# A four-layer gated decoder on one core: ternary feed-forward reordered with the next stage's small folds in it, first rows loaded in parts

## Chip, core and metric

One core of one Trainium2 chip runs the whole program in one launch. The metric is the device time in microseconds (us), lower is better. Engines are called by the profile's names: PE is TensorE (PEld its weight loads), DVE VectorE, ACT ScalarE, POOL GpSimd, SP the sync engine that issues the DMAs.

## The reference, cut to what matters

The input x has 16 sequences of 56 rows of 256 values. Four layers follow; each adds a gated attention and then a gated feed-forward, both on layer-normalised rows. The feed-forward of layer 1 is the ternary one:

```python
def h_bitlinear(x, w):
    xq = act_quant(fwht(x))       # Hadamard transform, then 8 bits per row: scale 127/max|x|, round, clip to -128..127
    wq = weight_quant(w)          # ternary weights, one scale per matrix
    return jnp.einsum('bsh,oh->bso', xq, wq)
gate = h_bitlinear(hidden_states, w_gate)   # 256 -> 1024
up = h_bitlinear(hidden_states, w_up)       # 256 -> 1024
return h_bitlinear(jax.nn.silu(gate) * up, w_down)   # 1024 -> 256
```

The attention of layer 2 needs, per head, the products of small matrices (`W_qr` with `W_kr`, and `w_kc_q` with `Wq`) before its queries can be computed; the kernel calls these products folds.

## The kernel before, in words

The 896 rows are 8 tiles of 112 rows. The program is a row of blocks with a barrier of all engines between two; in a block each engine runs its own list of instructions in order, and waits on semaphores that the others raise. The blocks that matter here are these.

`begin` (lines 355 to 391): SP loads x in one transfer, then the identity matrix and two rows of gates, then the weights of the first attention (`ahead.load`). DVE waits for all four of the first transfers (`came` at 64) and takes mean and variance of each tile (`take_moments`, lines 351 and 353), PE waits for the same and runs 8 matmuls that nobody reads (`keep_busy`, line 219). SP leaves the block only when all weights have landed.

`causal_attention` of layer 0 (from 418): POOL clears `values` (4096 words, line 478) and smaller buffers, then writes the masked keys (line 490), four `tensor_tensor` per pair of sequences, each kept until the scores two pairs before are done. DVE normalises the eight tiles (`scale_all`, line 267), PE turns each (line 310), ACT copies it (line 286), and PE then projects the queries (line 517).

`ternary_ffn` (from 1789). `rows(p)` on DVE scales two tiles of rotated rows (maximum, three small operations, two `tensor_scalar` that multiply and clip at 127, one that clips at -128 and adds the rounding constant). Then per tile t: PE computes gate and up (`inner`, eight matmuls, line 1864, four banks `ps_gu`), ACT takes silu of the gate half (line 1950), DVE multiplies with the up half (`product`, line 2013) and does the first level of a Hadamard transform of 1024 (`butterflies`, lines 1724 and 1725), POOL does two more levels (the same lines), PE turns the result (`turn_h`, 1877), ACT copies it (`take_h`, 1957), PE rotates it with a 128 x 128 Hadamard matrix (`rotate`, 1889), DVE quantises (`quantise` and `clip`, 2025 to 2039), ACT rounds to bf16 (1963), PE turns that (`turn_quantised`, 1899), ACT copies (1969), PE multiplies with the down weights (`down`, 1908), and DVE adds to x (`add`, 2043). `rotate`, `turn_quantised` and `down` each begin with three `keep_busy` matmuls. The order is written out by hand, and PE's is:

```python
                for i in range(2, NT + 3):
                    if i < NT:
                        inner(i)
                    if i < NT + 2:
                        turn_h(i - 2)
                        rotate(i - 2)
                    if i >= 3:
                        turn_quantised(i - 3)
                        down(i - 3)
```

On the side, POOL clears the buffers of the next stage's small weights `wqrT` and `wkrT` (line 172), and SP then loads these (six transfers, 1,024 KB) and two large ones (1,536 and 2,048 KB).

`queries_roped` of layer 2 (from 1161): PE first folds `wqrT` with `wkrT` in twelve steps into two halves of a PSUM bank (lines 1218 and 1221), ACT copies each to `z` (line 1275); only then PE folds the sixteen heads of `G` (line 1227), ACT takes the root for the norm (line 278) and casts `G` (line 1279), and DVE, after the moments (lines 253 and 256), takes the low part (line 1298), which lets PE go on four heads later.

## Time and profile before

| what | value |
|---|---|
| median of 3 runs | 1644.47 us (1644.42 to 1648.88) |
| the profiled execution | 1653.14 us, its span 1651.3 us, mean granted clock 0.976 |
| busy in the span | PE 1550.3, PEld 1239.0, DVE 906.1, ACT 648.8, POOL 668.3 us |
| `begin` and the attention of layer 0 up to the first scores | 0 to about 34 us |
| ternary feed-forward | about 645.6 to 745.6 us |
| roped queries of layer 2 | from 745.9 us |
| moved by DMA in the span | 154.47 MB, mean 94 GB/s |

Most of the span is the two long attentions of layers 1 and 2, which the change leaves alone. A time of the profile counts from the first instruction. A row of the timeline has the start, the length, the engine and the line, what is written and read, how many instructions were merged in it, and in brackets how long the engine had been idle and who ended that. "PEclk" is the granted TensorE clock as a share of 2.4 GHz, so 0.50 is 1.2 GHz.

### The profile page before, as it was taken

The page shows a single profiled execution, that of the slowest core. Times are in us where ns is not written, and L with a number is a line of the kernel's source. Part 1 is how long each engine was busy: PE and PEld are TensorE (multiplying, and loading weights), DVE is VectorE, ACT ScalarE, POOL GpSimd, SP SyncE. Part 2 cuts the span into 40 slices and gives each one's busy share as a digit, 9 for nine tenths or more (in the row PEclk, how much of TensorE's full clock was granted, in tenths as well). Part 3 has the DMA queues.
Part 4 walks back from the last instruction along what each step waited for, and adds up shares of the span by engine and source line. Part 5 has one row for each costly group of instructions (what it writes and reads, how often), then busy time and mean ns, then how long its engine had stood idle before and what let it go on. Part 6 is the DMA issues. An engine that isn't in the chain of part 4 may idle for free. (4 is left out here: it accounts for less than half of the span.)

```text
span 1651.3 us, 39610 instructions
## 1 busy us (share of the span) xinstructions
PE 1550.3 (94%) x17172; PEld 1239.0 (75%) x17184; DVE 906.1 (55%) x1648; ACT 648.8 (39%) x931; POOL 668.3 (40%) x482
## 2 busy tenths in 40 slices
PE   6889899999999998788998999999999999898998
PEld 3575688888888877676665888888888878645565
DVE  4950566665667626864555555565655253367212
ACT  3544344444444433344011544444454422144221
POOL 4405664465544100630975636644462011080101
PEclk9999899999999999998998999999999999999999
DMA  8006575644563122104123655355622030061402
GB/s 222 14 10 145 115 154 128 140 115 114 117 144 90 42 87 74 45 1 128 48 56 83 142 136 121 92 122 120 135 68 62 3 118 0 5 240 54 163 23 64
DMA packets 66413, 154.47 MB, mean 94 GB/s; under 512 B 14924, under 2 KB 44172, under 8 KB 65376
## 3 DMA queue, kind: packets, MB, share of 16 engines
q1 hardware_dynamic: 65472, 150.10, 36.2%
q8 instruction: 136, 2.23, 0.6%
q0 software_dynamic: 768, 1.84, 0.4%
q14 instruction: 37, 0.30, 0.1%
HBM read 87.51 MB, written 5.51 MB: 56 GB/s over the span
## 5 line engine op out<-in xcount | busy, mean ns | idle before, releaser
L1593 DVE TENSOR_REDUCE latent_psW<-latent_psW 128x1 f32<-128x500 f32 x654 | 418.1, 682 | 233.2 <-PE latent_psW L1488 232.7
L1571 ACT ACTIVATE latent_w<-latent_psS 125x896 f32<-125x896 f32 x384 | 351.7, 919 | 427.4 <-PE latent_psS L1506 423.8
L1516 PEld LDWEIGHTS latent_psO<-latent_val,latent_w 125*64 125x64 f32 x10752 | 323.8, 138 | 24.6 <-issue 11.1
L1516 PE MATMUL latent_psO<-latent_val,latent_w 125*64 125x65 f32 x10752 | 339.4, 223 | 0.0
L1505 PE MATMUL latent_psS<-latent_qA,latent_kA 128*125 128x448 f32 x768 | 290.6, 378 | 3.9 <-DVE latent_qB L1609 2.4
L1506 PE MATMUL latent_psS<-latent_qB,latent_kB 128*125 128x448 f32 x768 | 282.4, 368 | 0.0
L1488 PE MATMUL latent_psW<-latent_kA,latent_qA 128*128 128x500 f32 x654 | 214.5, 397 | 3.4 <-DMA latent_qA<-latent_qh 2.4
L1505 PEld LDWEIGHTS latent_psS<-latent_qA,latent_kA 128*125 128x125 f32 x768 | 143.6, 187 | 31.1 <-ACT latent_w L1571 4.6
L1506 PEld LDWEIGHTS latent_psS<-latent_qB,latent_kB 128*125 128x125 f32 x768 | 143.8, 187 | 19.9
L1488 PEld LDWEIGHTS latent_psW<-latent_kA,latent_qA 128*128 128x128 f32 x654 | 124.4, 191 | 20.3 <-DVE latent_psW L1593 5.8
L935 POOL TENSOR_TENSOR latent_rawT<-latent_rawT,latent_ropeT 128x1000 f32<-128x1000 f32 x48 | 110.8, 2334 | 34.0 <-DMA latent_rawT<-in_ctx_cols 22.0
L967 POOL TENSOR_TENSOR latent_val<-latent_raw,latent_turned_half 125x768 f32<-125x768 f32 x32 | 59.0, 1843 | 152.7 <-PE latent_psO L1516 150.2
L1452 POOL TENSOR_TENSOR latent_ql<-latent_q,latent_qh 128x448 fp32r<-128x448 f32 x32 | 36.4, 1141 | 156.0 <-ACT latent_qh L1562 155.9
L1318 POOL TENSOR_TENSOR q_u_roped<-q_u_roped 128x448 f32<-128x448 f32 x48 | 54.0, 1151 | 76.0 <-DVE q_u_roped L1308 75.8
L1308 DVE TENSOR_TENSOR q_u_roped<-q_ps_g,q_rope 128x448 f32<-128x448 f32 x96 | 53.2, 616 | 45.1 <-PE q_ps_g L1248 23.5
L958 POOL TENSOR_TENSOR latent_turned_half<-latent_raw,latent_rope 125x384 f32<-125x384 f32 x64 | 63.2, 1008 | 21.2 <-DMA latent_raw<-in_ctx 21.1
L1614 DVE RECIPROCAL latent_rec<-latent_psO 128x7 f32<-128x7 f32 x32 | 6.6, 205 | 115.0 <-PE latent_psO L1516 115.0
L950 POOL TENSOR_TENSOR latent_rawT<-latent_rawT,latent_high 128x1500 fp32r<-128x1500 f32 x16 | 54.3, 3391 | 18.6 <-ACT latent_high L979 18.6
L1673 PE MATMUL out_ps<-latent_fold,latent_q 128*112 128x256 f32 x256 | 59.1, 388 | 1.8 <-PEq L1399 1.8
L963 POOL TENSOR_TENSOR latent_raw<-latent_raw,latent_rope 125x768 f32<-125x768 f32 x32 | 59.1, 1848 | 2.4
L940 POOL TENSOR_TENSOR latent_rawT<-latent_rawT 128x500 f32<-128x500 f32 x48 | 59.3, 1263 | 0.0
L1673 PEld LDWEIGHTS out_ps<-latent_fold,latent_q 128*112 128x112 f32 x256 | 45.4, 181 | 11.6 <-issue 2.0
(399 smaller groups left out, 2201.7 us busy)
## 6 DMA issues: line engine op xcount, KB each, us to landing
latent_qA<-latent_qh SPq DMA_DIRECT2D x128, 112.0 KB, 2.6
latent_rawT<-in_ctx_cols SPq DMA_DIRECT2D x32, 375.0 KB, 5.2
latent_rawT<-in_ctx_cols SPq DMA_DIRECT2D x64, 187.5 KB, 5.8
latent_raw<-in_ctx SPq DMA_DIRECT2D x32, 375.0 KB
latent_kA<-latent_high SPq DMA_DIRECT2D x32, 375.0 KB, 4.2
latent_kB<-latent_high SPq DMA_DIRECT2D x32, 375.0 KB, 5.7
latent_kA<-latent_rawT SPq DMA_DIRECT2D x32, 375.0 KB, 6.2
experts_wgu<-in_L_gu SPq DMA_DIRECT2D x8, 1024.0 KB, 16.2
```

Of the source, the lines that this page charges most:

```text
L935: pool.tensor_tensor(x[:, :, at], x[:, :, at], self.ropeT[:, :, at], ALU.mult).then_inc(self.product, 1)
L940: pool.tensor_tensor(x[:, 0, at], x[:, 0, at], x[:, 1, at], ALU.add).then_inc(self.keys_roped, 1)
L958: last = pool.tensor_tensor(self.turned_half[:, :, lo:lo + 32], self.raw[b % 2][:, :, hi:hi + 32], self.rope[:, 1, :, lo:lo + 32], ALU.mult)
L963: pool.tensor_tensor(self.raw[b % 2][:, :, :], self.raw[b % 2][:, :, :], self.rope[:, 0, :, :], ALU.mult).then_inc(self.roped, 1)
L967: pool.tensor_tensor(self.val[b % 2][:, :, 0:DC], self.raw[b % 2][:, :, :], self.turned_half[:, :, :], ALU.add).then_inc(self.val_ready, 1)
L1488: pe.matmul((spare if alone and j % 2 else psW)[:, m, 0:THIRD], qA[u][:, j * 128:(j + 1) * 128], kA[u][:, n.part(m)], start=True, stop=Tru ...
L1505: pe.matmul(to[:, h, 0:GH], kA[u][:, at], qA[u][:, h * GH:(h + 1) * GH], start=True, stop=False)
L1506: last = pe.matmul(to[:, h, 0:GH], kB[u][:, at], qB[b % 2][:, h * GH:(h + 1) * GH], start=False, stop=True)
L1516: last = pe.matmul(sums[r:r + 64, c, :], w[t % ROUND][:, queries_of(c, r):queries_of(c, r) + 64], val[b % 2][:, t, :], start=(t == 0 and c ...
L1571: act.activation(w[t % ROUND][:, :].rearrange("p (h n) -> p h n", h=2), psS[0:KP, t % 2, :, 0:GH], ACT.Exp).then_inc(exp_done, 1)
L1593: dve.tensor_reduce(bank[:, THIRD + j:THIRD + j + 1], bank[:, 0:THIRD], mybir.AxisListType.X, ALU.max).then_inc(max_ready, 1)
L1673: last = pe.matmul(ps[0:TP, t % 2, 0:C], q[:, j, t * TP:(t + 1) * TP], fold[:, j, :], start=(j == 0), stop=(j == HP - 1))
```

## The change

Six edits.

1. `begin`: x comes in four transfers with a semaphore each, the identity between the first and the second; DVE takes the moments of a pair of tiles when its part is there, PE and ACT wait for the other three transfers.
2. `causal_attention`, layer 0: POOL no longer clears `values` first but between its fourth and fifth key product, and it begins the keys only when the eight normalised tiles are written (`norm.xn_ready`). Layer 3 keeps its order.
3. `ternary_ffn`, quantisation: the clip operations and one small operation per pair and per tile are left out, the scale being folded into the others; the product and the rounding constant are one `tensor_scalar`.
4. `ternary_ffn`, order: gate and up raise two semaphores, and silu waits for the gate alone; down of tile i-4 stands before rotate of tile i-2; the copies on ACT and the additions on DVE move accordingly; the last tile uses the banks of `ps_gu`; all `keep_busy` are left out but one of six before the last turn; all four `rows(p)` stand ahead of the first product.
5. The twelve folds of `wqrT` and `wkrT` move from `queries_roped` into `ternary_ffn`, six before gate(1) and six after the fourth turn of rows, on PE and ACT.
6. The small weights are loaded first and on a semaphore of their own.

```diff
@@ begin @@
-                sp.dma_start(g.x[:, :, :], d["x"].rearrange("(t p) c -> p t c", p=TP)).then_inc(came, 16)
-                sp.dma_start(g.ident[:, :], d["ident"]).then_inc(came, 16)
+                for p in range(NT // 2):
+                    sp.dma_start(g.x[:, 2 * p:2 * p + 2, :], rows[:, 2 * p:2 * p + 2, :]).then_inc(x_came[p], 16)
+                    if p == 0:
+                        sp.dma_start(g.ident[:, :], d["ident"]).then_inc(came, 16)
...
-                    take_moments(dve, g, t, came, 64, stats_done)
+                    take_moments(dve, g, t, x_came[t // 2], 16, stats_done)
@@ causal_attention, gpsimd @@
-                pool.memset(values[:, :, :, :, :], 0.0).then_inc(zeroed, 1)
+                if layer:
+                    pool.memset(values[:, :, :, :, :], 0.0).then_inc(emptied, 1)
...
+                if not layer:
+                    pool.wait_ge(norm.xn_ready, NT)
                 pool.wait_ge(taken, KV)
                 for n in range(2 * B):
                     b, c = n // 2, n % 2
+                    if n == 4 and not layer:
+                        pool.memset(values[:, :, :, :, :], 0.0).then_inc(emptied, 1)
@@ RopedWeights, new @@
+    def fold_tensor(self, pe, n):
+        k, t = n // 3, n % 3
+        flat = lambda v, e: self.wqrT[:, v, :, :, :].rearrange("p j e i -> p (j e i)")[:, e]
+        if n == 0:
+            pe.wait_ge(self.small_came, 16 * len(self.small_loads))
+        if n >= 2:
+            pe.wait_ge(self.z_ready, n - 1)
...
+        last.then_inc(self.z_done, 1)
+    def fold_scalar(self, act, n):
+        act.wait_ge(self.z_done, n + 1)
+        act.copy(self.z[:, n, :, :, :].rearrange("p v e n -> p (v e n)"), self.bank[n % 2][:, 0:256]).then_inc(self.z_ready, 1)
@@ queries_roped: the twelve fold steps on PE and their copies on ACT are gone @@
-                for n in range(3 * QUADS):
...
-                    act.copy(z[:, n, :, :, :].rearrange("p v e n -> p (v e n)"), ps_q[:, 0, n % 2, 0:256]).then_inc(z_ready, 1)
@@ ternary_ffn, tensor @@
+                for p in range(NPX - 1):
+                    rotate_rows(p)
                 turn_rows(0)
-                inner(0)
-                rotate_rows(2)
+                gate_part(0)
+                up_part(0)
+                rotate_rows(NPX - 1)
                 turn_rows(1)
-                rotate_rows(3)
                 turn_rows(2)
-                inner(1)
+                pe.wait_ge(x_taken, NT)
+                for n in range(0, 6):
+                    ahead.fold_tensor(pe, n)
+                gate_part(1)
+                up_part(1)
                 turn_rows(3)
-                for i in range(2, NT + 3):
+                for n in range(6, 3 * (NH // 4)):
+                    ahead.fold_tensor(pe, n)
+                for i in range(2, NT + 1):
                     if i < NT:
-                        inner(i)
-                    if i < NT + 2:
-                        turn_h(i - 2)
-                        rotate(i - 2)
+                        gate_part(i)
+                    turn_h(i - 2)
+                    if i < NT:
+                        up_part(i)
+                    if i >= 4:
+                        down(i - 4)
+                    rotate(i - 2)
                     if i >= 3:
                         turn_quantised(i - 3)
-                        down(i - 3)
+                turn_h(NT - 1)
+                down(NT - 3)
+                rotate(NT - 1)
+                for t in (NT - 2, NT - 1):
+                    turn_quantised(t)
+                    down(t)
@@ ternary_ffn, vector @@
-                    step(dve.tensor_scalar(r2[:, at], r2[:, at], 127.0, 1.0 / 32.0, ALU.mult, ALU.mult))
-                    between()
...
-                    dve.tensor_scalar(ys[:, u, :].rearrange("p (a n) -> p a n", a=2), ps_y[0:TP, :, :], r2[:, at], 127.0,
-                                      ALU.mult, ALU.min).then_inc(y_taken, 1)
+                    dve.tensor_scalar(ys[:, u, :].rearrange("p (a n) -> p a n", a=2), bank, r2[:, at], ROUND,
+                                      ALU.mult, ALU.add).then_inc(y_taken, 1)
...
-                    dve.tensor_scalar(ys[:, u, :], ys[:, u, :], -128.0, ROUND, ALU.max, ALU.add).then_inc(y_clipped, 1)
...
-                rows(0)
-                rows(1)
-                rows(2)
+                for p in range(NPX):
+                    rows(p)
                 product(0)
-                rows(3)
                 product(1)
-                for i in range(2, NT + 3):
+                for i in range(2, NT + 1):
                     if i < NT:
                         product(i)
...
+                    if i >= 4:
+                        add(i - 4)
+                    quantise(i - 2)
+                add(NT - 3)
+                quantise(NT - 1)
+                add(NT - 2)
+                add(NT - 1)
```

## Rows read from the trace of the kernel before

**Rows 1.** Waits of SP's queue, first 60 us: total us, times, longest

```profile
SPq L365 <- DMA xattn_w__6_54<-in_headmask: 6.4, 1, 6.4
...
SPq L365 <- PEq L365: 0.3, 1, 0.3
```

**Rows 2.** Timeline of the first 35 us: start us, us, engine, line

```profile
12.94 3.51 POOL L478 MEMSET xattn_values<- 128x4096 f32 x1 [12.49 <-POOLq L365]
...
18.32 8.28 POOL L490 TENSOR_TENSOR latent_q<-xattn_kT,xattn_w__6_54 128x512 f32<-128x512 f32 x8
...
24.83 8.15 PE L517 MATMUL xattn_ps_a<-all_xnT,xattn_w__3_51 128*128 128x448 f32 x16 [0.43 <-ACT all_xnT L286]
```

**Rows 3.** Line 267 in the first layer, 14 to 25 us: ns min/median/max

```profile
L267 DVE TENSOR_SCALAR all_xn<-all_x,xattn_ln_rstd,xattn_ln_shift x8: 394/1128/1590, 15.0 to 22.6; 112x256 f32<-112x256 f32 x8
```

**Rows 4.** Line 267 in the third layer, 758 to 763 us

```profile
L267 DVE TENSOR_SCALAR all_xn<-all_x,q_ln_rstd,q_ln_shift x8: 404/406/411, 759.2 to 761.5; 112x256 f32<-112x256 f32 x8
```

**Rows 5.** Windows: stretch, length, busy us by engine, PEclk, DMA share, GB/s

```profile
25.00:29.00 4.00, 4.00 (x6) 1.85 (x7) 0.00 (x0) 0.54 (x1) 1.60 (x2) 0.55 0.96 217
...
650.00:655.00 5.00, 4.38 (x30) 3.44 (x29) 4.35 (x14) 1.98 (x3) 0.00 (x0) 1.00 1.02 170
```

**Rows 6.** Timeline, one turn of the ternary loop on PE and ACT

```profile
699.07 1.80 PEld L1889 LDWEIGHTS ffn_ps_y<-ffn_w__82_8816,ffn_hT 128*112 128x112 f32 x16 [0.74 <-ACT ffn_hT L1957]
...
701.47 0.51 PEld L1899 LDWEIGHTS ffn_ps_t<-ffn_w_identb,ffn_yq 112*128 112x128 bf16 x8
...
702.17 0.91 ACT L1969 COPY ffn_yqT<-ffn_ps_t 128x896 bf16<-128x896 bf16 x1 [2.11 <-PE ffn_ps_t L1899]
...
703.13 0.83 PEld L1908 LDWEIGHTS ffn_ps_t<-ffn_w_wb,ffn_yqT 128*112 128x112 bf16 x8 [0.46 <-ACT ffn_yqT L1969]
...
703.94 1.53 PEld L1864 LDWEIGHTS ffn_ps_gu<-ffn_w_wb,ffn_xqT 128*112 128x112 bf16 x8
...
705.97 1.12 ACT L1950 ACTIVATE ffn_h<-ffn_ps_gu,ffn_su 112x1024 f32<-112x1024 f32 x1 [2.90 <-PE ffn_ps_gu L1864]
...
706.99 0.90 ACT L1957 COPY ffn_hT<-ffn_ps_t 128x896 f32<-128x896 f32 x1
```

**Rows 7.** Line 1275, the copies of the twelve folds: ns min/median/max, first and last start

```profile
L1275 ACT COPY q_z<-q_ps_q x12: 372/372/373, 746.6 to 753.2; 128x256 f32<-128x256 f32 x12
```

**Rows 8.** Timeline, start of the roped queries

```profile
745.91 2.71 DVE L253 BATCH_NORM_STATS2 all_stats<-all_x 112x6 f32<-112x256 f32 x8 [0.32 <-PEq L1819]
...
748.54 0.62 DVE L256 BATCH_NORM_AGGREGATE all_mv<-all_stats 112x2 f32<-112x6 f32 x8
...
755.07 1.60 ACT L1279 CAST q_G<-q_ps_g 128x384 fp32r<-128x384 f32 x4
```

**Rows 9.** Timeline: third turn of rows, gate and up of tile 2, product of tile 2

```profile
660.33 0.37 PE L1853 MATMUL ffn_ps_t<-ffn_w_identb,ffn_xq 112*128 112x112 bf16 x4 [1.54 <-ACT ffn_xq L1938]
...
669.60 3.63 PE L1864 MATMUL ffn_ps_gu<-ffn_w_wb,ffn_xqT 128*112 128x512 bf16 x8 [1.38 <-DVE ffn_h L2013]
...
674.42 1.29 DVE L2013 SCALAR_TENSOR_TENSOR ffn_h<-ffn_ps_gu,ffn_su,ffn_h 112x1024 f32<-112x1024 f32 x1 [3.51 <-ACT ffn_h L1950]
```

**Rows 10.** Costliest lines, 698.2 to 715.9 us, two tiles: count, busy, mean ns

```profile
L1725 POOL TENSOR_TENSOR ffn_h<-ffn_h 112x512 f32<-112x512 f32 x4 | 5.1, 1271 | 0.3
...
L2013 DVE SCALAR_TENSOR_TENSOR ffn_h<-ffn_ps_gu,ffn_su,ffn_h 112x1024 f32<-112x1024 f32 x2 | 2.6, 1283 | 0.4 <-ACT ffn_h L1950 0.4
...
L1724 DVE TENSOR_TENSOR ffn_h<-ffn_h 112x512 f32<-112x512 f32 x2 | 1.4, 692 | 0.1
```

**Rows 11.** Timeline, a GpSimd and a VectorE butterfly at once

```profile
675.02 1.27 POOL L1725 TENSOR_TENSOR ffn_h<-ffn_h 112x512 f32<-112x512 f32 x1
...
675.74 1.10 DVE L1724 TENSOR_TENSOR ffn_h<-ffn_h 112x512 f32<-112x512 f32 x1
```

**Rows 12.** Timeline of the tail: product of tile 7 and the last addition

```profile
715.99 1.28 DVE L2013 SCALAR_TENSOR_TENSOR ffn_h<-ffn_ps_gu,ffn_su,ffn_h 112x1024 f32<-112x1024 f32 x1 [0.19 <-ACT ffn_h L1950]
...
745.11 0.48 DVE L2043 SCALAR_TENSOR_TENSOR all_x<-ffn_ps_t,ffn_s,all_x 112x256 f32<-112x256 f32 x1 [4.87 <-PE ffn_ps_t L1908]
```

More of the change, by code:

```diff
@@ L360, in begin @@
         came = a.sem("came")
+        x_came = [a.sem(f"x_came{p}") for p in range(NT // 2)]
         stats_done = a.sem("stats_done")
@@ L374, in _ @@
                 ahead.wait(sp)
+                sp.wait_ge(came, 48)
             @block.tensor
             def _(pe):
-                pe.wait_ge(came, 64)
+                pe.wait_ge(came, 48)
                 keep_busy(pe, g, ps[:, 0:128], 8)
@@ L1272, in _ @@
             def _(act):
-                for n in range(3 * QUADS):
-                    act.wait_ge(z_done, n + 1)
-                    act.copy(z[:, n, :, :, :].rearrange("p v e n -> p (v e n)"), ps_q[:, 0, n % 2, 0:256]).then_inc(z_ready, 1)
                 norm.root(act)
@@ L1977, in _ @@
                 take_rows(2)
+                for n in range(0, 4):
+                    ahead.fold_scalar(act, n)
+                round_rows(3)
+                for n in range(4, 6):
+                    ahead.fold_scalar(act, n)
                 silu(1)
-                round_rows(3)
                 take_rows(3)
-                for i in range(2, NT + 3):
+                for n in range(6, 3 * (NH // 4)):
+                    ahead.fold_scalar(act, n)
+                for i in range(2, NT + 1):
+                    if i >= 4:
+                        take_quantised(i - 4)
                     if i < NT:
                         silu(i)
-                    if i < NT + 2:
-                        take_h(i - 2)
+                    take_h(i - 2)
                     if i >= 3:
                         round_quantised(i - 3)
-                        take_quantised(i - 3)
+                take_quantised(NT - 3)
+                take_h(NT - 1)
+                for t in (NT - 2, NT - 1):
+                    round_quantised(t)
+                    take_quantised(t)
             @block.vector
@@ L2579, in program @@
             clear_semaphores(nc)
-            ahead = roped_weights(nc, g, d)
+            ahead = RopedWeights(nc, g, d)
             ternary_ffn(nc, g, w, ahead)
+            ahead.small.close()
             w.ctx.close()
```

201 lines of the change are left out of this document (105 added, 96 removed).

## The prediction

> **What bounds the kernel now.** The change touches three stretches, and I read each at the wait that ends last in it.
>
> The start. The view of SP's own waits shows that SP held the first block open: it waited 6.4 us for the last weights of the first attention and only 0.3 us more at the barrier [rows 1]; the next block opened at 12.94. The single load of x, for which DVE waits, is therefore only just behind. In the next block GpSimd clears `values` and then writes keys, 12.94 to 26.6, and in just that time DVE normalises eight tiles [rows 2]: they take 1128 ns (median, 1590 at most) where the same operation takes 406 ns in a stretch in which GpSimd does nothing [rows 3, 4]. The projection of the queries starts behind the last tile at 24.83 and takes 8.15 us, part of it at a granted clock of 0.55, after a stretch in which PE had waited for DVE between tiles [rows 2, 5].
>
> The ternary loop. In the timeline one tile takes 8.87 us (two products of DVE lie so far apart), and no engine is full. The loop closes over PE and ACT, because PE takes its list in order [rows 6]: from rotate's start 699.07 to the turn 701.47 it is 2.40 (keep-busy matmuls among it), to ACT's copy 0.70, to down 0.96, to gate and up 0.81, to silu 2.03, to the copy of the next tile 1.02, and that copy ends at 707.88, 0.9 later. Together 8.8. The work on DVE and POOL hangs beside it.
>
> The roped queries. ACT's twelve copies of folds start from 746.6 to 753.2, and the first cast of `G` follows at 755.07, although the moments are there at 749.16 [rows 7, 8].
>
> **Begin.** Three more issues on SP, about 0.5 us each, lie ahead of the weights, but the transfers run far behind the issues. The moments end some 4 us sooner, and SP's wait for the weights then ends the block: it saves the 0.2 to 0.3 by which SP came first. Taken: 0.2; bounds -0.5 (the issues delay the weights) to 0.5.
>
> **Keys behind the normalised rows.** DVE's eight tiles go from 1128 to 406 ns each, or 0.33 from start to start [rows 4]: 15.0 to 17.8. Then the pair of PE and ACT paces the turns: 0.41 on PE and 0.35 on ACT over two buffers give 0.43 a tile (estimate), the last copy ends at 20.7 instead of 24.8, so 4.1 saved. PE has no gaps to speak of in that time, so I take the projection at full clock, 16 times 0.376, 6.1 instead of 8.15: 2.0 more. GpSimd's keys: it began at 18.32 because it cleared first; now it begins at 17.9. Four keys take 4.1, the clearing 3.5 and the next four 4.1 [rows 2]: ready at 22.0 and 29.7. The first scores then want theirs at 27.6, the second at 30.6. Both are covered, the second by only 0.9. The clearing ends at 25.6, its reader comes near 31. Four transfers of folding weights wait for POOL's next clearing and now leave 3 us sooner; nobody waits. Taken: 6.1; bounds 4.0 (the clock falls as before) and 6.5.
>
> **The ternary stage, entry.** No product stands between the four `rows`, and each loses a small operation and a clip, some 0.6 a pair. The third turn of rows was at 660.33 [rows 9]; I put it at 658.0 (estimate). Then twelve fold steps, 0.59 each by the copies' starts [rows 7], gate and up of tile 1 (1.6), gate of tile 2, the turn of h and up (0.8, 0.8, 1.2): 658.0 + 7.1 + 1.6 + 2.8 = 669.5 for product 2, which stood at 674.42 behind matmuls at half clock (3.63 for eight, against 1.89 at full) [rows 6, 9]. Saved: 4.9. The folds are covered by POOL's 5.4 us for tile 0, which PE awaits anyway; without that cover they cost their 7.1. Their six small loads, 1,024 KB, go first from about 650 at the 170 GB/s of that window [rows 5], so they land near 656.5, 1.5 before fold 0. If they come at 661, all shifts by 3.
>
> **The steady loop.** Gate before turn, and down before rotate, cut PE's ring: its own work is 1.62 + 0.8 + 1.73 + 0.45 + 0.81 = 5.4 a tile, all keep-busy gone. DVE's list is product 1.32, two butterflies 1.34, addition 0.40, maximum 1.27, two small 0.38, write 1.19, small 0.24 = 6.1 (lengths by product and butterfly [rows 10], maximum and write taken like the product for their 1024 elements). POOL's is four times 1.345, 5.4. All three fit below 8.87, so what counts is who stands in whose way. With DVE at 6.1 a tile, its two butterflies fall on the end of POOL's work on the tile before. The one place where they met shows what then happens: POOL's ran 675.02 to 676.29, DVE's began at 675.74 and lasted 1.10 instead of 0.69, it ended 0.55 after POOL's [rows 10, 11]. So I let POOL's 5.4 and DVE's 1.4 exclude each other: 6.8 a tile. From product 2 to product 7 that is 34.0 instead of 41.6 (715.99 - 674.42 [rows 9, 12]): 7.6 saved. Ends: 6.1, if only that one row was slow, and 8.87.
>
> The Trainium skill, page "SBUF — State Buffer", section "Who interferes with whom", has this as a rule: a VectorE instruction with two SBUF inputs and a GpSimd instruction that reads SBUF use one port pair, and the second to start fully blocks until the first is through. The row above agrees. Read to the letter it gives the 6.8; without it the sum would be 3.5 us lower over five tiles.
>
> **The tail.** From product 7 on the last tile is a plain chain: product and blocked butterflies 3.5, POOL 5.4, turn 1.0, copy 0.95, rotate 2.05, maximum to write 2.95, round 1.2, turn 0.7, copy 0.95, down 1.2, that is 19.9 instead of 29.1 [rows 6, 10, 12], because tiles 5 and 6 no longer stand in line for `x_done` and the keep-busy: 9.2 saved. The last addition comes at 669.5 + 34.0 + 19.9 = 723.4. Stage: 21.7.
>
> **Roped queries.** With the folds gone, ACT loads its table during the moments and takes the root when they end, 3.26 after the stage's start, so the first cast of `G` comes at about 3.5 instead of 9.16 [rows 8]: 5.6 saved of the 7.2 removed. But PE now idles 2 us after four heads, and once more during the normalisation; I take 1.0 back for a fall of the clock. Taken: 4.6; bounds 3.0 and 5.7.
>
> **Sum.** 0.2 + 6.1 + 21.7 + 4.6 = 32.6. On the profiled execution (1653.14, span 1651.3) that gives 1620.5; it lies 8.7 above the median of the runs, and I take the difference off the median: 1644.47 - 32.6 = 1611.9, so 1612.
>
> **Rivals.** A measurement of this kernel can tell 0.3%, 4.9 us, from no change.
>
> Forecast (0.60): as summed.
>
> No exclusion (0.14): DVE alone sets 6.1 to 6.2; 3.5 less in the loop, 1 in the tail, 1607. For it: elsewhere DVE's product and write lie beside POOL at full speed. Against: [rows 11].
>
> The gains come in part (0.20): the small loads are late (3), the clock falls in the folds, in `G` or in the projection (2 each), or POOL and DVE block each other in both directions (0.4 a tile, 2 in all): 1612 + 8 = 1620. For it: the eight matmuls of tile 2 ran at half clock after PE had stood almost idle, and PE will idle in places again. Against: it takes all of them at once.
>
> PE at half clock all through the ternary stage (0.04), because keep-busy held it up: eight gate and up matmuls took 3.63 against 1.89 [rows 6, 9], so 5.4 a tile become 10.4, 1.5 above the 8.87 of now, 12 over eight tiles; the twelve folds cost 6.5 more. The stage is then 18.5 slower, the rest saves 8 to 9: about 1654. It decides once a tile takes over 8.87, that is if PE is slow for more than two thirds of it. Against: gaps in the new list stay below 1 us, and a PE busy for 4.38 of 5 us held the full clock [rows 5]. The Trainium skill, page "TensorE: Matmul & The Clock Gate", Part 1, states that throttled is the default and that activity lifts it; the trace agrees in both directions, and this rival is that rule at its worst.
>
> No change to speak of (0.02): a later stage takes the gain back; nothing in the profile shows such a link, as the blocks are parted by barriers.
>
> **How the numbers follow.** Faster by over 0.3% holds the first three: 0.94. Slower 0.04, same 0.02. The range leaves out 0.2 at most: down to 1603 (no exclusion, no fall of the clock, 1606, less 3 for the spread of the runs, which was 4.5 before), up to 1624 (partial gains 1620, plus 4).
>
> **What would show it.** Line 267 near 400 ns in the first layer and keys starting at 17.9. The projection at 16 x 0.38. Products of tiles 3 to 7 spaced 6.8, with the first butterfly longer than 0.69 and ending just behind a POOL operation; 6.1 and 0.69 would be the second case. Fold 0 at 658 without a wait for a DMA. The stage about 78 us long instead of 99.7. First cast of `G` 3.5 after the stage's start. A PEclk of 0.5 in the ternary loop, or a product spacing above 8, would make the prediction wrong.

## Result and the profile after

The changed kernel takes 1624.05 us (median of 4 runs, 1620.69 to 1630.3) beside 1646.68 for the kernel before on the same chip (1644.42 to 1650.83). The ratio is 0.9846, 95% interval 0.9822 to 0.987: 25.4 us faster (21.4 to 29.3) where 32.6 were forecast. The time stands on the upper edge of the range, 1624, while the median of before is 2.2 above the 1644.47 that the forecast started from. The same kernel timed again beside the last experiments gave 0.9846 once more. One of the ten executions of the kernel with the keys alone took 3059.65 us, in a slow state, and is not in its ratio.

The profiled execution took 1626.06 us, its span 1624.3 (before 1653.14 and 1651.3). From here on, times inside a stage are counted from the stage's own start (a plus sign), because what is gained earlier shifts everything behind it.

The start, in the timeline of the kernel after (start, duration, engine, line, operation; in the bracket the idle time before and what ended it):

```profile
7.00 0.43 SPq L190 DMA_DIRECT2D xattn_w__6_54<-in_headmask  x1
9.31 0.18 DVE L353 BATCH_NORM_AGGREGATE all_mv<-all_stats 112x2 f32<-112x6 f32 x1
13.92 0.11 POOL L486 MEMSET xattn_qT<- 128x16 f32 x1 [13.48 <-POOLq L366]
15.99 2.67 DVE L267 TENSOR_SCALAR all_xn<-all_x,xattn_ln_rstd,xattn_ln_shift 112x256 f32<-112x256 f32 x8
18.80 4.04 POOL L501 TENSOR_TENSOR latent_q<-xattn_kT,xattn_w__6_54 128x512 f32<-128x512 f32 x4 [3.09 <-DVE all_xn L267]
21.93 7.97 PE L528 MATMUL xattn_ps_a<-all_xnT,xattn_w__3_51 128*128 128x448 f32 x16 [0.44 <-ACT all_xnT L286]
30.77 0.38 PE L547 MATMUL xattn_ps_a<-xattn_maskb,xattn_identb 128*128 128x512 bf16 x1 [0.86 <-ACT xattn_qT L625]
```

The moments end at 9.5 instead of 12.7, but the next block opens at 13.92, not at 12.94 [rows 2]: nobody needed them sooner, and the last weights now come later. The eight normalisations take 2.67 us together instead of 8.70, and GpSimd's keys begin right behind them. The projection starts 8.0 behind the block's opening instead of 11.9, yet it takes 7.97, not the 6.1 of the forecast.

The ternary stage starts at 642.44. Its entry, the same view:

```profile
656.15 0.71 PE L1200 MATMUL ffn_ps_y<-q_small_wkrT,q_small_wqrT 128*128 128x128 f32 x4 [0.29 <-DVE ffn_xs L2074]
657.56 2.08 PE L1200 MATMUL ffn_ps_y<-q_small_wkrT,q_small_wqrT 128*128 128x128 f32 x8
...
664.27 1.25 PE L1200 MATMUL ffn_ps_y<-q_small_wkrT,q_small_wqrT 128*128 128x128 f32 x8
...
669.36 1.28 DVE L2083 SCALAR_TENSOR_TENSOR ffn_h<-ffn_ps_gu,ffn_su,ffn_h 112x1024 f32<-112x1024 f32 x1 [3.25 <-PE ffn_ps_gu L1900]
```

and the granted clock (PE busy, PEclk, DMA share, GB/s) there, with one stretch of the loop:

```profile
642.00:645.00 3.00, 2.52 (x8) 0.74 0.00 0
657.00:660.00 3.00, 3.00 (x20) 0.52 0.99 421
663.00:666.00 3.00, 3.00 (x33) 1.00 0.00 0
675.00:678.00 3.00, 2.32 (x25) 1.00 0.00 0
```

Fold 0 (656.15) waits for DVE's rows and not for a load: the last small load landed at 654.12. The clock was down at the stage's start as well (0.74). The same eight fold matmuls take 2.08 at a granted clock of 0.52 (near 1.2 GHz) and 1.25 at 1.00 (2.4 GHz). Product 2 comes at +26.9; before it was +28.8 [rows 9].

One turn of the steady loop, and ahead of it DVE's first butterfly of an earlier one:

```profile
677.10 1.63 DVE L1755 TENSOR_TENSOR ffn_h<-ffn_h 112x512 f32<-112x512 f32 x1
...
690.27 1.27 POOL L1756 TENSOR_TENSOR ffn_h<-ffn_h 112x512 f32<-112x512 f32 x1
690.85 1.24 DVE L1755 TENSOR_TENSOR ffn_h<-ffn_h 112x512 f32<-112x512 f32 x1
692.12 0.69 DVE L1756 TENSOR_TENSOR ffn_h<-ffn_h 112x512 f32<-112x512 f32 x1
692.89 1.28 POOL L1755 TENSOR_TENSOR ffn_h<-ffn_h 112x512 f32<-112x512 f32 x1 [1.35 <-DVE ffn_h L1756]
```

DVE's first butterfly begins under GpSimd's last operation, which ends at 691.54, and is through 0.55 later; the second takes its 0.69; GpSimd starts again after 1.35 idle. 5.35 and 1.35 are 6.7, and products 3 to 7 stand 6.68, 7.07, 6.67 and 6.68 apart (8.87 before, from product 4 on). In the turns before the first addition (0.48) DVE has less to do, its butterfly begins earlier and takes 1.63, and the spacing is the same: there the exclusion sets the pace and not DVE's list. The 7.07 is the turn in which the first addition comes in. From product 7 (702.88) to the last addition (724.21) it is 21.3. The stage lasts 82.6 instead of 100.3, barriers included: 17.8 saved.

The roped queries start at 725.01:

```profile
728.51 1.60 ACT L1310 CAST q_G<-q_ps_g 128x384 fp32r<-128x384 f32 x4
735.83 4.17 PE L1262 MATMUL q_ps_g<-q_w__93_9153,q_w__94_9154 128*128 128x192 f32 x24 [2.05 <-DVE q_G_low L1329]
```

The first cast of `G` is at +3.5, where 9.16 stood [rows 8]. The first wide matmul (of the query projection) is at +25.6 instead of +33.2.

### The profile page after: what moved, and what is told of

It is laid out like the page before. It is cut to its first block and busy times, and to the rows that moved or that the text cites. A ratio compares the mean times of both kernels' runs of the same rounds, so it can differ in the third digit from the quotient of the medians.

```text
span 1624.3 us, 39337 instructions
## 1 busy us (share of the span) xinstructions
PE 1530.7 (94%) x17028; PEld 1221.2 (75%) x17040; DVE 891.4 (55%) x1624; ACT 649.1 (40%) x931; POOL 667.8 (41%) x482
## 5 line engine op out<-in xcount | busy, mean ns | idle before, releaser
L1547 PEld LDWEIGHTS latent_psO<-latent_val,latent_w 125*64 125x64 f32 x10752 | 323.9, 138 | 25.2 <-issue 11.6
L1536 PEld LDWEIGHTS latent_psS<-latent_qA,latent_kA 128*125 128x125 f32 x768 | 143.4, 187 | 31.1 <-ACT latent_w L1602 4.6
L1339 DVE TENSOR_TENSOR q_u_roped<-q_ps_g,q_rope 128x448 f32<-128x448 f32 x96 | 53.2, 617 | 45.7 <-PE q_ps_g L1282 24.1
```

What stands on the lines that cost most here:

```text
L1536: pe.matmul(to[:, h, 0:GH], kA[u][:, at], qA[u][:, h * GH:(h + 1) * GH], start=True, stop=False)
L1547: last = pe.matmul(sums[r:r + 64, c, :], w[t % ROUND][:, queries_of(c, r):queries_of(c, r) + 64], val[b % 2][:, t, :], start=(t == 0 and c ...
```

## Experiments

Each kernel was timed against the kernel before (medians of before 1649.2 to 1650.44 us beside them). "Cost" below is the difference to the ratio of the changed kernel, 0.9846, times 1650: a thousandth is 1.65 us, and the intervals reach 2.5 to 5.5 us to either side. Against the changed kernel only the clip and the keep-busy below are clear of noise by their times alone; for the others the time is a hint and the trace decides.

**x in one load again** (`begin` as before).

```diff
-                for p in range(NT // 2):
-                    sp.dma_start(g.x[:, 2 * p:2 * p + 2, :], rows[:, 2 * p:2 * p + 2, :]).then_inc(x_came[p], 16)
+                sp.dma_start(g.x[:, :, :], d["x"].rearrange("(t p) c -> p t c", p=TP)).then_inc(came, 16)
```

> The changed kernel with its first block as before: x in one load, moments behind it. Theory (issue order): the last weights land some 7 us after SP has issued them, and three issues fewer in front put that issue back from 7.0 to 5.6 us; the next block opens at 12.9 to 13.0 instead of 13.9, all later steps keep their distances, total 1.0 us below the changed kernel. Rival A (bytes): the landing is set by the volume, the block opens at 13.9 as in the changed kernel and the total stays. Rival B (moments): DVE's moments, which begin only when all of x is there, end last and the block opens later than 13.0.

Ratio 0.9849 (0.9818 to 0.988). In its timeline the last weights are issued at 5.60 and the block opens at 12.75; the moments end at 12.5. That is the theory's opening, but no gain shows in the total. All traces together say more. With one load the block opened at 12.94, 12.75, 12.65 and 12.56; with four parts at 13.92, 12.97, 14.80, 13.69, 13.37, 13.14, 13.07, 12.65 and 13.05. The means are 12.7 and 13.4, but the ranges overlap, and the changed kernel's second profile opened at 12.65 with its last weights issued as late as 6.98. That loading in parts costs 0.7 is a hint and not shown.

**x issued by ACT** (and no longer by SP).

```diff
+                for p in range(NT // 2):
+                    act.dma_start(g.x[:, 2 * p:2 * p + 2, :], rows[:, 2 * p:2 * p + 2, :]).then_inc(x_came[p], 16)
                 act.wait_ge(came, 48)
```

> The changed kernel with the four loads of x issued by ACT instead of SP, beside SP's loads of weights. Theory (issue order on SP sets the landing of the last weights): SP issues the last weights at about 5.1 us instead of 7.0, the next block opens near 12.5 instead of 13.9, total 1 to 1.5 below the changed kernel. Rival A (the volume sets it; the changed kernel's other executions opened between 13.0 and 14.8 with the same issues): opening anywhere from 12.9 to 14.8, total unchanged. Rival B (two queues at once delay x): DVE's moments end last and open the block after 13.

Ratio 0.9841 (0.9815 to 0.9867). SP issued its last weights at 5.61, and the block opened at 13.09. So an earlier issue alone doesn't bring the landing forward by as much: rival A. What sets it (order, volume, chance) stays open.

**The keys alone, on the kernel before.**

```diff
+                if not layer:
+                    pool.wait_ge(norm.xn_ready, NT)
                 pool.wait_ge(taken, KV)
...
+                    if n == 4 and not layer:
+                        pool.memset(values[:, :, :, :, :], 0.0).then_inc(emptied, 1)
```

> The kernel before with one part alone: in the first layer GpSimd waits for the normalised rows before its keys, and clears the values after four keys. Theory: the eight normalisations fall from 1128 to about 400 ns each, the projection of the queries starts 4.1 us sooner after the block's opening (11.9 to about 7.9) but still takes 8 us because the clock falls; the first scores come 4.0 us sooner and the total is 4.0 below the kernel before. Rival A (the forecast on record): the projection runs at full clock, 6.1 us, and 6.1 are saved. Rival B: part of the gain of the changed kernel in this stretch came from its moments being done early; alone the keys save under 3.

Ratio to before 0.9988 (0.9973 to 1.0003), so 2 us, with an interval that takes in no change. In the trace the normalisations are short again, but now the first matmuls of the block run at half clock and the projection at full:

```profile
12.84 5.55 PE L514 MATMUL xattn_ps_a<-xattn_w__2_50,xattn_w__1_49 128*128 128x512 f32 x8 [1.00 <-PEq L365]
22.29 6.28 PE L523 MATMUL xattn_ps_a<-all_xnT,xattn_w__3_51 128*128 128x448 f32 x16 [0.44 <-ACT all_xnT L286]
```

The eight took 3.91 in the profile of before and the projection 8.15 [rows 2]. The first scores come +16.6 behind the opening (20.9 before, 16.9 in the changed kernel).

**The keys undone, on the changed kernel** (the same lines taken out of it).

> The changed kernel with GpSimd's clearing and keys back beside the normalisation. Theory (GpSimd and DVE shut each other out there): the eight normalisations take 1128 ns each again, the projection starts 11.9 after the block's opening instead of 8.0, the first scores 18.8 to 20.9 instead of 14.9, total 4 to 6 above the changed kernel. What it tells besides: whether the projection at half clock (8.15 us) belongs to this slow normalisation, with PE waiting between tiles (then first scores at 20.9), or falls there by chance (then 6.28 us and 19.0).

Ratio 0.9855 (0.9836 to 0.9874), a cost of 1.5, not clear of noise. The timeline of this kernel shows why it is so little:

```profile
13.24 5.56 PE L513 MATMUL xattn_ps_a<-xattn_w__2_50,xattn_w__1_49 128*128 128x512 f32 x8 [1.24 <-PEq L366]
15.13 5.57 DVE L267 TENSOR_SCALAR all_xn<-all_x,xattn_ln_rstd,xattn_ln_shift 112x256 f32<-112x256 f32 x8
19.51 8.09 POOL L495 TENSOR_TENSOR latent_q<-xattn_kT,xattn_w__6_54 128x512 f32<-128x512 f32 x8 [0.97 <-ACT xattn_kT L608]
22.70 6.28 PE L522 MATMUL xattn_ps_a<-all_xnT,xattn_w__3_51 128*128 128x448 f32 x16 [0.44 <-ACT all_xnT L286]
```

PE's first eight matmuls fell to half clock, so GpSimd got its last operand at 19.43 and wrote keys only from 19.51; by then seven of the eight normalisations had begun, and DVE took 5.57 for the eight, not 8.70. The first scores stand at +16.8, as in executions with the keys moved and the same fall. The collision that the forecast priced from one trace is thus worth 0 to 6 us by the traces, depending on where the clock falls.

**The folds and their small loads back in the roped queries.**

```diff
-                for n in range(0, 6):
-                    ahead.fold_tensor(pe, n)
                 gate_part(1)
                 up_part(1)
                 turn_rows(3)
-                for n in range(6, 3 * (NH // 4)):
-                    ahead.fold_tensor(pe, n)
...
+                for n in range(3 * QUADS):
+                    act.wait_ge(z_done, n + 1)
+                    act.copy(z[:, n, :, :, :].rearrange("p v e n -> p (v e n)"), ps_q[:, 0, n % 2, 0:256]).then_inc(z_ready, 1)
                 norm.root(act)
```

> The changed kernel with the twelve folds and their small loads back at the start of the roped queries. Theory (the folds lie on PE's path in the ternary entry): product 2 comes 2.5 to 4 us sooner after the stage's start than the 26.9 of the changed kernel, because PE reaches the turn of tile 0 when GpSimd has it ready instead of 2.8 later and gate 1 is not queued behind six folds; the spacing of products 3 to 7 stays 6.7; the first cast of G comes 9.2 after the roped stage's start instead of 3.5, the next step 7.5 later. Total 3.5 to 5 above the changed kernel. Rival A (forecast: GpSimd's 5.4 us for tile 0 cover the folds): product 2 stays at 26.9 and the total is 7.5 above. Rival B (PE colder without the folds): matmuls of tile 2 at half clock, product 2 at 27 or later.

Ratio 0.9883 (0.985 to 0.9916), a cost of 6.1. Product 2 is at +25.4, the first cast at +9.16, the first wide matmul, that is the first of the query projection, at +31.5 (+25.6 in the changed kernel). So the roped queries pay 5.9 and the ternary stage gets back 0 to 1.5: the two kernels with folds at full clock (x in one load, and the changed kernel's second profile) have product 2 at +25.46 as well. The folds are free where PE keeps its clock, as the forecast said; in the changed kernel's own profile they cost 1.5, the fall of the clock among them.

**Gate of tile 1 ahead of most folds** (on PE; ACT's list follows).

```diff
-                for n in range(0, 6):
+                for n in range(0, 2):
                     ahead.fold_tensor(pe, n)
                 gate_part(1)
                 up_part(1)
+                for n in range(2, 6):
+                    ahead.fold_tensor(pe, n)
                 turn_rows(3)
```

> The changed kernel; in the ternary entry only two folds stay ahead of gate and up of tile 1, the other ten come behind. Theory (product 1 is late, 19.5 us after the stage's start at full clock and 20.9 with a fall of it, because six folds stand before it; GpSimd then waits 1.8 us for tile 1): product 1 comes at 17 to 18, GpSimd goes from tile 0 to tile 1 without a gap, product 3 and all after it come 1 to 2 sooner after the stage's start; total 1 to 2 below the changed kernel. Rival A (PE's sum of work sets product 2 whatever the order): product 1 sooner, products 2 to 7 unchanged at 25.4 (26.9 where the clock falls in the folds) and on. Rival B (the folds behind gate 1 delay the turn of tile 0): products 2 and on later than in the changed kernel.

Ratio 0.986 (0.9832 to 0.9889), a cost of 2.3 or none. Product 1 comes 5.0 behind product 0 (5.6 in the kernels whose folds ran at full clock), product 2 comes 13.4 behind it (13.1 in the changed kernel's profile, where the clock fell too), product 3 19.1 (19.5). Beyond product 1 at most 0.4 is gained: rival A.

**Half of the product left in PSUM.**

```diff
-                    dve.scalar_tensor_tensor(out=h[:, u, :].rearrange("p (n m) -> p n m", n=2), in0=ps_gu[0:TP, 2:4, :],
...
+                        last = dve.scalar_tensor_tensor(out=ps_gu[0:TP, 3, :] if n else half, in0=ps_gu[0:TP, 2 + n, :],
+                                                        scalar=su[:, 1, t:t + 1], in1=half, op0=ALU.mult, op1=ALU.mult)
...
+                    low, high = h[:, u, 0:512], ps_gu[0:TP, 3, :]
+                    step(dve.tensor_tensor(h2[:, u, 0:512], low, high, ALU.add))
```

> The changed kernel; in the ternary loop DVE's product is made in two halves, the second of which stays in PSUM, so that DVE's two butterflies read one operand from SBUF and one from PSUM instead of two from SBUF. Theory (DVE's butterflies with two SBUF operands and GpSimd's shut each other out): the first butterfly falls from 1.25 to 1.6 us to about 0.7 and no longer ends behind a GpSimd operation; the spacing of products 3 to 7 falls from 6.7 to 6.1 to 6.3 (DVE's own list), the last tile gains 0.6 more, total 2.5 to 4 below the changed kernel. Rival A (the order of PE and ACT sets the pace): the butterflies get short, DVE waits longer elsewhere, spacing stays 6.7. Rival B (the slow butterfly is GpSimd's load on SBUF as such, whatever DVE reads): the butterflies stay at 1.2 or more.

Ratio 0.9822 (0.9789 to 0.9855), 4.0 gained, not clear of noise by itself. DVE and GpSimd at the same place of its loop:

```profile
691.51 0.75 DVE L2085 SCALAR_TENSOR_TENSOR ffn_h<-ffn_ps_gu,ffn_su,ffn_h 112x512 f32<-112x512 f32 x1
692.30 0.76 DVE L2085 SCALAR_TENSOR_TENSOR ffn_ps_gu<-ffn_ps_gu,ffn_su,ffn_h 112x512 f32<-112x512 f32 x1
693.09 0.69 DVE L2094 TENSOR_TENSOR ffn_h<-ffn_h,ffn_ps_gu 112x512 f32<-112x512 f32 x1
...
692.26 1.27 POOL L1756 TENSOR_TENSOR ffn_h<-ffn_h 112x512 f32<-112x512 f32 x1
```

The butterfly of 693.09 lies half under GpSimd's operation (to 693.53) and takes 0.69. The products stand 5.99, 5.98, 6.37, 6.38 and 6.38 apart, 31.1 for the five instead of 33.5 in the profile of the changed kernel and 34.1 in its second. The tail takes 19.5, without a fall of the clock; of that gain 0.3 at most is the edit's, as the same tail without the edit takes 19.8 at full clock. All 16 butterflies of this trace take 0.69. The exclusion goes with DVE's second operand in SBUF; the rest of DVE's list then sets 6.4, of which 0.2 is the product's second instruction.

The Trainium skill, page "SBUF — State Buffer", section "Who interferes with whom", says that a VectorE instruction with at most one SBUF input, outside the two-port modes, doesn't contend with GpSimd. This trace agrees: 0.69 against 1.24.

**The clip back in the loop.**

```diff
+                    dve.wait_ge(y_taken, t + 1)
+                    dve.tensor_scalar(ys[:, u, :], ys[:, u, :], -128.0, ROUND, ALU.max, ALU.add).then_inc(y_clipped, 1)
```

> The changed kernel with the second, clipping pass of DVE over the 1024 quantised values of a tile back in the loop (0.79 us in the trace of before). Theory (DVE's list is full at 6.7 us a tile, the 0.55 of its blocked butterfly among them): spacing of products 3 to 7 from 6.7 to 7.4 or 7.5, the last tile 0.8 longer, the total 4 to 6 above the changed kernel. Rival A (the ring of GpSimd's 5.35 and DVE's two butterflies 1.35 sets the pace and DVE has room): spacing stays 6.7, only the tail is longer, total within 1.5. Rival B (DVE a little late shifts its butterflies clear of GpSimd, which removes the blocking): spacing 6.9 to 7.0, total 1 to 2 above.

Ratio 0.9886 (0.9867 to 0.9905), a cost of 6.6. From product 3 on the spacing is 7.50, the theory's. Its rows are the surprise:

```profile
695.66 1.27 POOL L1755 TENSOR_TENSOR ffn_h<-ffn_h 112x512 f32<-112x512 f32 x1
696.14 1.34 DVE L2103 TENSOR_SCALAR ffn_ys<-ffn_ys 112x1024 f32<-112x1024 f32 x1
697.01 1.60 POOL L1756 TENSOR_TENSOR ffn_h<-ffn_h 112x512 f32<-112x512 f32 x1
697.64 1.28 DVE L2083 SCALAR_TENSOR_TENSOR ffn_h<-ffn_ps_gu,ffn_su,ffn_h 112x1024 f32<-112x1024 f32 x1
698.96 0.69 DVE L1755 TENSOR_TENSOR ffn_h<-ffn_h 112x512 f32<-112x512 f32 x1
```

DVE runs 0.8 later, its butterfly is clear of GpSimd (0.69), but now the clip, from SBUF to SBUF with one operand, meets GpSimd and takes 1.34 instead of the 0.78 that most turns of before have for it (0.69 where GpSimd stood still). And GpSimd pays too: its operation of 697.01 begins under the clip and takes 1.60 instead of 1.27, as one does under the clip of each of six tiles. The block moved; it did not go. The tail is 24.1, 2.8 longer, with a granted clock of 0.75 and 0.68 in the two stretches of 6 us from 706 on.

**Keep-busy back in the loop** (three calls each before the rotations, the turns of quantised rows and the down projections of the loop).

```diff
+                        keep_busy(pe, g, ps_y[:, 0, 0:128], 3)
                     pe.wait_ge(hT_ready, t + 1)
...
+                    keep_busy(pe, g, ps_t[:, 1, 0:128], 3)
                     pe.wait_ge(yqT_ready, t + 1)
```

> The changed kernel with three keep-busy calls put back in front of each rotation, each turn of quantised rows and each down projection of the ternary loop (0.83 us for each three in the trace of before). Theory (they cost what they last, because the new order fills PE): PE's own list grows from 5.4 to 7.9 us a tile, the spacing of products 3 to 7 goes from 6.7 to about 7.9, and the total is 6 to 9 above the changed kernel (1630 to 1633). Rival A (they lie in PE's waits for DVE and GpSimd, 1.3 us a tile): spacing 6.7 to 7.0, total unchanged; then the gain of the loop is the new order's alone. Rival B (they hold the clock and pay for themselves in the tail): total at or below the changed kernel.

Ratio 0.9912 (0.9888 to 0.9936), a cost of 10.9. The last three products are 8.28 to 8.29 apart, 0.4 more than the 7.9 of PE's sum; PE is busy for 5.7 to 5.9 of every 6 us there, and DVE waits 1.1 us a tile for its rotation. The tail takes 24.6.

```profile
693.19 0.94 PE L219 MATMUL ffn_ps_t<-all_ident 128*128 128x128 f32 x6
693.96 1.04 PE L1958 MATMUL ffn_ps_t<-ffn_w_wb,ffn_yqT 128*112 128x256 bf16 x8
694.83 0.83 PE L219 MATMUL ffn_ps_y<-all_ident 128*128 128x128 f32 x6
695.50 1.91 PE L1935 MATMUL ffn_ps_y<-ffn_w__82_8821,ffn_hT 128*112 128x128 f32 x16
697.25 0.83 PE L219 MATMUL ffn_ps_t<-all_ident 128*128 128x128 f32 x6
697.45 1.23 DVE L2097 TENSOR_REDUCE ffn_r<-ffn_ps_y 112x1 f32<-112x1024 f32 x1 [1.12 <-PE ffn_ps_y L1935]
```

PE needs none of it to keep its clock in the loop: from 666 to 708 the changed kernel has 1.00 without. No run takes keep-busy out of the old order, so how much of the loop's gain is the new order's and how much only the missing keep-busy isn't shown.

**The addition between product and butterflies.**

```diff
                                              op0=ALU.mult, op1=ALU.mult).then_inc(product_done, 1)
+                    between()
                     dve.wait_ge(product_done, t + 1)
```

> The changed kernel; in the ternary loop DVE's addition of tile i-4 stands between its product and its butterflies of tile i, in the time in which the first butterfly would be blocked by GpSimd, instead of behind them. Theory (the tail is 1.4 longer than forecast because PE stands 1.5 us before the turn of tile 6, waiting for that addition, and then runs down(5) and the rotation of tile 6 at half clock): the turn of tile 6 starts 1.5 to 1.8 sooner, the tail from product 7 to the last addition falls from 21.3 to 19 to 20; the spacing stays 6.7, because GpSimd's 5.35 and the two butterflies of DVE still exclude each other. Total 1.5 to 2.5 below the changed kernel. Rival A (the butterflies then start later and GpSimd with them): spacing 7.1, total 1 to 2 above. Rival B (GpSimd's last tile is the tail's limit): tail 20.5 to 21.3, total unchanged.

Ratio 0.9843 (0.9825 to 0.9861): no difference that can be timed. From product 3 on the spacing is 6.67 to 6.69, without the one of 7.07, and the tail 20.1. PE in the tail (turn of tile 6, down of tile 5, rotation of tile 6), first of this kernel, then of the changed kernel's second profile, then of the kernel with the keys undone, whose ternary code is the changed kernel's:

```profile
701.48 0.96 PE L1922 MATMUL ffn_ps_t<-all_ident,ffn_h 112*128 112x112 f32 x8 [1.04 <-POOL ffn_h L1756]
703.43 1.08 PE L1956 MATMUL ffn_ps_t<-ffn_w_wb,ffn_yqT 128*112 128x256 bf16 x8 [0.99 <-ACT ffn_hT L2018]
704.72 2.00 PE L1933 MATMUL ffn_ps_y<-ffn_w__82_8821,ffn_hT 128*112 128x128 f32 x16 [0.21 <-DVE ffn_ys L2101]
```

```profile
700.88 0.96 PE L1922 MATMUL ffn_ps_t<-all_ident,ffn_h 112*128 112x112 f32 x8 [1.50 <-DVE all_x L2106]
702.84 1.96 PE L1956 MATMUL ffn_ps_t<-ffn_w_wb,ffn_yqT 128*112 128x256 bf16 x8 [0.99 <-ACT ffn_hT L2018]
704.58 2.71 PE L1933 MATMUL ffn_ps_y<-ffn_w__82_8821,ffn_hT 128*112 128x128 f32 x16
```

```profile
702.00 0.96 PE L1916 MATMUL ffn_ps_t<-all_ident,ffn_h 112*128 112x112 f32 x8 [1.50 <-DVE all_x L2100]
703.95 1.08 PE L1950 MATMUL ffn_ps_t<-ffn_w_wb,ffn_yqT 128*112 128x256 bf16 x8 [0.99 <-ACT ffn_hT L2012]
704.87 1.91 PE L1927 MATMUL ffn_ps_y<-ffn_w__82_8820,ffn_hT 128*112 128x128 f32 x16
```

In the second, PE stood 1.50 for the addition, and its next two steps took 1.96 and 2.71 instead of 1.08 and 2.00. In the third it stood the same 1.50, kept its clock (1.08 and 1.91), and the tail took 19.8. So the wait for the addition costs the tail nothing and doesn't by itself bring the fall. The turn itself comes only 0.5 sooner after product 7, not the 1.5 expected: GpSimd is then the one it waits for. Nor does the edit hold the clock: the kernel with three edits below has the early addition too, and there it fell.

**The changed kernel again.**

> The changed kernel unaltered, as the yardstick for the two others on the same chip and for the falls of the clock. Theory (the three stretches at half clock in its first profile, the projection 7.97 instead of 6.28 us, the rows 1.47 and the folds 1.46, are not fixed to these places): the second profile has at least one of them at full clock, product 0 at 12.4 or 13.8 and product 2 at 24.0, 25.5 or 26.9 after the stage's start. Rival (they belong to this program): all three lie where they lay, product 2 at 26.9.

Ratio 0.9846 (0.9827 to 0.9864). The projection took 6.28, but the block's first matmuls ran at half clock; product 0 is at +13.8, product 2 at +25.5. So the falls aren't fixed to the program.

**Three edits together** (x in one load, half of the product in PSUM, the addition early).

> The changed kernel with three edits together: x in one load, half of the product left in PSUM for DVE's butterflies, and the addition between product and butterflies. Theory: each keeps its own gain: the first block opens 0.9 sooner (12.8), the spacing of products 3 to 7 is 6.0 to 6.4 (1.6 to 2.4 in all), the tail from product 7 is 19.5 or less; the ternary stage takes 75 to 78 us instead of 80.2 to 82.6; total 4 to 6 below the changed kernel. Rival A (clock): a PE that idles more in the shorter loop falls to half clock there, and the stage stays above 79. Rival B: addition and butterflies in a row fill DVE, spacing 6.4 and no gain in the tail, total 3 below.

1619.87 us, ratio 0.9825 (0.9803 to 0.9847), against 0.9846 for the changed kernel beside it: faster by 3.5 to 4.7, with intervals that overlap. The block opens at 12.56, spacing 5.98 to 6.25, stage 78.2 with a tail of 21.2 in which the clock fell (0.72 from 700 to 706). By its ratio it is the fastest against before together with the PSUM edit alone, from which it can't be told.

## Where the clock fell

The same code in different executions, by the timelines. Full-clock values stand first; a cell with another number has a fall in it.

| stretch | at full clock | with a fall | fell in |
|---|---|---|---|
| opening of the block to first scores, keys moved | 14.9 to 15.2 | 16.6 to 17.9 | 5 of 12 traces |
| stage start to product 0 | 12.4 | 13.8 | 8 of 12 |
| product 0 to product 2 (folds as in the change) | 11.6 | 13.1 | 2 of 10 |
| product 7 to last addition | 19.5 to 20.1 | 21.2 to 21.5 | 7 of 10 |
| last six heads of `G` | 4.17 | 5.8 to 5.9 | 6 of 14 |

The first row counts the traces with the keys moved, the second those with the ternary order of the change. The third leaves out the two with another order of folds, the fourth the two with the clip or keep-busy back. Three of the ten in the fourth row have other edits in the loop (half of the product in PSUM 19.5, the addition early 20.1, both 21.2); of the seven without, six fell, and the kernel with the keys undone took 19.8. In the stretch to product 0 the granted clock tells them apart: 0.53 in the first 3 us of the kernel with one load (13.8), 1.00 in the kernel with keep-busy in its loop (12.4), with the same code there. The changed kernel's first profile has a fall in the first four rows, together 6.3 us.

## Why the prediction was right or wrong

**Direction and most of the mechanism** were right: faster, at 0.9846, by the ternary stage and the roped queries, as named. What the keys give isn't clear of noise in the total, and the first block gave nothing. The outcome lies nearer to the rival that had 0.20, the gains in part (1620, that is 24.5 saved), than to the sum that had 0.60. That rival named the falls of the clock in the projection and in the folds, which came, and late small loads, which didn't. That 1624.05 falls on the edge of the range and not beyond it is luck: leaving out a single one of the four executions moves the median by 2 us.

**Begin** (0.2, bounds -0.5 to 0.5): no gain came. The opening moved back by 1.0 in the two profiles and by 0.7 on average over the traces, which puts the step "the transfers run far behind the issues" in doubt. But it ran from 12.65 to 14.80 with the same issues, and the two runs on it show no gain in time, so the cause stays open.

**Keys behind the normalised rows** (6.1): mis-sized. The rows are as forecast: normalisation 407 ns, start of the projection 3.9 sooner (4.1), and where the clock held, the projection took 6.28 (6.1) and the scores came 6.0 sooner than in the profile of before. But the profile of before was a dear execution. With keys and normalisation in collision the scores stand at +20.9 there and at +16.8 in the other trace of it, and the timed runs give 2.0 (on the kernel before) and 1.5 (on the changed one). The step that failed is the price taken from a single execution, with its own fall of the clock in it. By the middle values this is 4 of the missing 7; both runs have intervals that reach from no gain to over 4 us.

**Ternary entry** (4.9): at full clock product 2 comes at +24.0 (four traces); the forecast's 669.5 is +23.9. That it fits so well is partly luck: the third turn of rows came at +11.6 and not at +12.4, and from there it took 12.4 and not 11.5. In the profile there are two falls, 1.5 each, and 1.9 was saved. The guard against that was in the rival "gains in part", which named the clock and the folds.

**Steady loop** (6.8 a tile, 34.0 for five): 33.5, and 34.1 where all stood at full clock. The exclusion was shown by taking one SBUF operand away: the butterflies fell from 1.24 or more to 0.69. With it DVE is busy for 5.8 of every 6 us, so that the 0.8 of the clip came through at once. The forecast that DVE and GpSimd would fit at 6.1 "if only that row was slow" is refuted.

**Tail** (19.9): 21.3 in the profile, 19.8 where PE kept its clock with the same ternary code. The sum was right for a PE at full clock. The step "plain chain" failed where the clock fell: the down projection of tile 5 and the rotation of tile 6 (1.96 and 2.56 instead of 1.08 and 1.91) then hold PE, and the turn of tile 7, the chain's next link, starts at 713.21 although GpSimd was through with that tile at 711.57. Counted from product 7 it comes 1.5 later than at full clock. PE's wait for the addition of tile 4 is in both and costs nothing.

**Folds, small loads:** free at full clock, no wait for a load. Right, though the margin was small: at full clock the last load landed at +11.3 to +11.6 and fold 0 began at +12.2.

**Roped queries** (4.6, of which -1.0 for the clock): 5.7 to the first cast, and 5.5 to 6.0 to the first wide matmul where the last six heads of `G` ran at full clock in both (+25.6 to +25.9 beside +31.4 to +31.5). The two profiles show 7.6, because the six heads were at half clock in that of before and not in the other. The fee for the clock is a matter of chance: the heads fell in 5 of 11 traces with the folds moved, with the first wide matmul then at +27.4 or +27.5, and in 1 of 3 without. Timed, the move of the folds is worth 6.1.

**The sum.** Timed or measured by stage it is now: keys 1.5 to 2, ternary stage with its folds 17.8 (the two profiles; 19.5 as the mean of five traces against two), roped queries 5.9 to 7.6, begin 0 to -1.0, together 24 to 29 beside the measured 25.4. At full clock everywhere the ternary stage is 78.8 long (the kernel with the keys undone; forecast 78), so the forecast described an execution without a fall, and among the traces only the kernel with keep-busy back has none in the five stretches of the table. From the first wide matmul to the end it is 871.8 to 876.7 us in the traces, with the same code behind it: 872.3 to 873.2 in the three kernels whose folds are not moved, 874.8 as the mean of the eleven others. Whether the change costs 2 us there is open.

## What to carry over

Price a collision or a projection from more than one execution if the granted clock is below 1 anywhere near it: one fall is 1.5 to 2 us, as large as a good edit. Where two engines exclude each other over SBUF, look at how many operands of DVE lie there: leaving one in PSUM parted them here, while moving DVE's list by 0.8 only moved the block to the next instruction. In the tail the fall cost 1.5 because the chain's next link stood in PE's line behind the slow matmuls: look there first. Whether transfers that gate a barrier gain by an earlier issue isn't shown here.

## What was not expected

The falls come in the same places of the program but not in each execution: the same ternary entry has product 2 at +24.0, +25.5 or +26.9. The stretch between two stages that no edit touches (from the first scores to the ternary stage) took 607.5 to 613.9 us.

DVE's one-operand pass from SBUF to SBUF was stretched by GpSimd as well, 0.78 to 1.34 and 0.41 to 1.13. DVE pays more often, but not alone: GpSimd's butterfly took 1.59 to 1.60 instead of 1.27 once in the second profile of the changed kernel and seven times with the clip back, each time begun while a stretched operation of DVE was still under way. In the trace of before one took 1.69 (from 688.90) behind a clip that had begun at 688.76 and kept its 0.69: there GpSimd alone paid. The Trainium skill has this too, in the same section of "SBUF — State Buffer": `tensor_scalar` can enter a two-port mode that contends with GpSimd; the rows agree. The pass over 1024 elements that reads PSUM takes 1.28 in each turn.
